# Rebuilding the projection stage and scoring four cosine heads at once in row tiles of 32 rows

## The reference

```python
xn = layernorm(x)
out = x + cosine_attention(xn) + block(xn)
# cosine_attention: 16 heads of 8; q and k scaled to unit length; scores = g_scale * q.k; softmax over all 1024 keys
# block: y = xn + causal_attention(rmsnorm(xn)*g1)   # 16 heads of 8, 4 key/value heads, rotary, softmax over keys <= query
#        y + moe(rmsnorm(y)*g2)                      # 4 experts of 384, the best 2 per token, silu(x w1)*(x w3) w2
```

## Time and profile before

| | us |
|---|---|
| median of 3 runs | 706.04 (703.66 to 708.68) |
| the profiled execution | 704.94 |
| its span, first to last instruction | 703.2 |

### The profile page before, as it was taken

How to read it: one execution, slowest core, us unless ns; L and a number is a source line. 1 busy time by engine, 2 the same in 40 slices (tenths; PEclk the granted TensorE clock), 3 DMA queues, 4 the chain that set the end, 5 groups by cost and what they waited for, 6 DMA issues and landing times.

```text
span 703.2 us, 11124 instructions
## 1 busy us (share of the span) xinstructions
PE 625.5 (89%) x4088; PEld 275.9 (39%) x4088; DVE 368.6 (52%) x1042; ACT 461.1 (66%) x520; POOL 106.1 (15%) x245
## 2 busy tenths in 40 slices
PE   0665887999999999999999999999998689999996
PEld 0433332333333333333333333333332445556654
DVE  6588385556556555555555654655521534344333
ACT  1444674888889888889888888988988332222221
POOL 8237000210210210130021021021002200000000
PEclk9979799999999999999999999999999889999999
DMA  3003411220311302124332030230000000000000
GB/s 84 4 1 61 70 20 17 47 45 4 61 19 28 58 6 47 30 34 92 100 52 38 10 62 12 35 48 16 1 3 1 1 0 1 15 1 16 0 16 15
DMA packets 19189, 20.61 MB, mean 29 GB/s; under 512 B 8128, under 2 KB 15552, under 8 KB 19136
## 3 DMA queue, kind: packets, MB, share of 16 engines
q1 hardware_dynamic: 16736, 19.62, 15.9%
q10 hardware_dynamic: 2400, 0.30, 0.3%
HBM read 3.84 MB, written 1.05 MB: 7 GB/s over the span
## 4 chain that ended last, share of the span: by engine, by line
PE 77%; DVE 12%; ACT 4%; issue 2%; SPq 2%; DMA 1%; POOL 0%; DVEq 0%; ACTq 0%
PE ps L1076 27%; PE ps L1057 19%; PE ps L1157 6%; PE ps L1008 6%; PE ps L1143 5%; PE ps L1144 5%; PE ps L1037 2%; DVE masked_scores L736 2%; DVE neg_piece L740 2%; PE ps L1031 2%; ACT probs L599 2%; DVE out_t L816 2%; SPq L361 2%; DVE probs L677 1%; DMA x_tok<-in_x 1%
## 5 line engine op out<-in xcount | busy, mean ns | idle before, releaser
L599 ACT ACTIVATE probs<-ps 128x1024 f32<-128x1024 f32 (+2 forms) x416 | 395.3, 991 | 80.1 <-PE ps L1057 75.8
L736 DVE CUSTOM_DVE_ANT_0 masked_scores<-ps,mask_q 128x384 bf16<-128x384 f32 (+3 forms) x256 | 111.6, 488 | 70.2 <-PE ps L1008 69.6
L1076 PE MATMUL ps<-probs,v_cos_pad 128*32 128x512 f32 x1024 | 138.1, 612 | 0.0
L1057 PE MATMUL ps<-q_cos_t,k_cos_t 64*128 64x512 f32 x512 | 122.9, 479 | 8.0 <-DMA q_cos_t<-parts_t_cos 6.2
L505 POOL TENSOR_SCALAR_AFFINE_SELECT probs<-probs 128x512 f32<-128x512 f32 x64 | 40.4, 637 | 412.9 <-ACT probs L599 412.9
L1057 PEld LDWEIGHTS ps<-q_cos_t,k_cos_t 64*128 64x128 f32 x512 | 48.2, 186 | 128.3 <-ACT probs L599 78.8
L740 DVE TENSOR_REDUCE neg_piece<-ps 128x1 f32<-128x512 f32 x128 | 82.1, 685 | 23.0 <-PE ps L1008 22.9
L637 ACT ACTIVATE probs<-ps 128x512 f32<-128x512 f32 x48 | 28.6, 597 | 96.3 <-PE ps L1144 84.9
L1076 PE MATMUL ps<-probs,v_causal_pad 128*32 128x512 f32 (+3 forms) x768 | 81.7, 498 | 0.3 <-POOL probs L505 0.3
L1057 PE MATMUL ps<-q_causal_t,k_causal_t 64*128 64x512 f32 (+3 forms) x384 | 73.5, 408 | 7.3 <-DMA q_causal_t<-neg_max_t 4.1
L1008 PE MATMUL ps<-k_causal_t,q_causal_t 33*128 33x512 f32 (+3 forms) x384 | 64.1, 371 | 17.3 <-DVE neg_piece L740 9.2
(11 more groups left out here) (131 smaller groups left out, 429.4 us busy)
## 6 DMA issues: line engine op xcount, KB each, us to landing
q_cos_t<-parts_t_cos SPq DMA_DIRECT2D x64, 64.0 KB
q_causal_t<-parts_t_rope SPq DMA_DIRECT2D x64, 64.0 KB
k_cos_t<-parts_t_cos SPq DMA_DIRECT2D x32, 64.0 KB
k_cos_t<-parts_t_cos SPq DMA_DIRECT2D x64, 32.0 KB
parts_cos<-in_w SPq DMA_DIRECT2D x2, 768.0 KB, 5.6
x_tok<-in_x SPq DMA_DIRECT2D x4, 256.0 KB, 4.4
k_causal_t<-parts_t_rope SPq DMA_DIRECT2D x16, 64.0 KB
k_causal_t<-parts_t_rope SPq DMA_DIRECT2D x32, 32.0 KB
```

Source lines behind the costliest of these rows:

```text
L599: act.activation(step_probs(n), step_scores(n), ACT.Exp).then_inc(probs_ready, 1)
L736: ins = dve.tensor_tensor_reduce(out=masked_scores[:, head % 2, at:at + keys], in0=scores, in1=mask_q[:, BANK - keys:BANK], scale=-1.0, sc ...
L1057: ins = pe.matmul(slot(n)[:, i, at:at + width], rounded(keys[:, j * P:(j + 1) * P]), rounded(queries[:, q0:q0 + width]), start=True, stop= ...
L1076: ins = pe.matmul(acc[32 * h:32 * h + 32, lo:], v, unit_probs(n)[:, h, lo:], start=j == 0, stop=True, skip_group_check=True)
```

## The change

**Projection.** `xn` is written at once (no staging, no copy on ACT). `xn_t`, `rope_in` and `rope_a` get two buffers. The second rope halves go from DVE to POOL. The clearing of the second pair of buffers on POOL moves behind the projection. 28 products of the identity come first on PE. The reciprocal of the norms is taken before their bound.

**First cosine rows.** Instead of the 20 DMAs, PE transposes the first parts into banks 6 and 7, ACT copies them, and products with matrices of zeros and ones (`choose_q`, `choose_k`, made on POOL) put the rows where they belong. ACT copies the first 512 tokens' rows, DVE the others. The loop starts when chunk 3's projections are read; ACT waits for the rest of chunk 3 at its steps 2, 4 and 6. The constant shift becomes the bias of the cosine exponentials. The rope jobs for iteration 1 go from steps 3 and 4 to 12 and 15 of iteration 0; its maxima start two steps earlier.

**Cosine steps from iteration 1 on** (`grouped`). A head takes 32 rows of the array instead of 64: pair (0,1) rows 0 and 64, pair (2,3) rows 32 and 96. There are three slots, banks 0 and 1, 2 and 3, 5 and 6, so step n waits for exponential n-3. All jobs in these steps use bank 7 alone. A value unit stands four steps behind its second score (three before). The 8 max jobs of two banks become 16 "one" jobs of one head and one bank, and some jobs stand behind the value unit of their step (place 1).

```diff
+def grouped(step):
+    return STEPS <= step < ITERS * STEPS and step % STEPS < COS_STEPS
...
+        last = it * STEPS + LAST_STEP[u]
+        step = last + (3 if on_diagonal(u) else 2)
+        if grouped(last) and grouped(last + 4):
+            step = last + 4
...
-EARLY_STEPS = (30, 32, 34, 35, 41, 42, 46, 48, 49, 51)
-MAX_STEPS = (8, 10, 12, 14, 16, 18, 19, 22)
+EARLY_STEPS = (32, 34, 35, 37, 41, 42, 46, 48, 49, 51)
+ONE_STEPS = ((1, 0), (3, 0), (5, 0), (7, 0), (7, 1), (9, 0), (11, 0), (11, 1), (13, 0), (15, 0), (15, 1), (17, 0), (19, 0),
+             (19, 1), (21, 0), (23, 0))
...
+        out += [(9, 1, ("out", it - 1, 3)), (23, 1, ("out", it, 0)), (25, 0, ("neg_max", it, 0))]
+        if more:
+            out += [(3, 1, ("rope", it + 1, 0)), (5, 1, ("rope", it + 1, 1))]
+            out += [(step, place, ("cos", it + 1, n)) for n, (step, place) in enumerate(((27, 1), (29, 1)))]
...
+SLOTS = ((0, 1), (2, 3), (5, 6))
+AUX_BANKS = (5, 6, 7)
...
+        elif grouped(step):
+            bank = AUX_BANKS[2]
+        else:
+            bank = AUX_BANKS[(AUX_BANKS.index(FILL_BANK[-1]) + 1) % 3]
...
+        SLOT.append(_step % 3 if grouped(_n) else _step % 2)
...
+                if kind == "one":
+                    pair, fill = MAX_JOBS[a // 2]
+                    i, at = a % 2, 0
+                    for t, key, keys, diagonal in MAX_FILLS[fill]:
+                        at += keys
+                        rows = slice(i * HEAD_ROWS, i * HEAD_ROWS + PRODUCT_ROWS)
+                        ins = pe.matmul(aux(m)[:, at - keys:at],
...
                     if kind == COS:
-                        keys, queries = k_cos_t[it % 2][rows, a, :], q_cos_t[it % 2][rows, a, :]
+                        first = cos_row(h) if grouped(n) else i * HEAD_ROWS
+                        rows = slice(first, first + (PRODUCT_ROWS if grouped(n) else HEAD_ROWS))
+                        keys, queries = k_cos_t[it % 2][rows, :], q_cos_t[it % 2][rows, a, :]
...
+            for half in range(2):
+                for i, choice in enumerate((choose_q[:, 0, :], choose_q[:, 1, :], choose_k[:, :])):
+                    if half:
+                        pe.wait_ge(first_rows_copied, i + 1)
+                    pe.matmul(ps[:, 5 + i, :], rounded(choice), rounded(parts_t["cos"][:, half * BANK:(half + 1) * BANK]),
+                              start=True, stop=True).then_inc(first_rows_in_psum, 1)
+            warm_up(WARM_UP, 4)
...
             for n in range(END + 1):
                 if n < ITERS * STEPS:
                     score_step(n)
-                for job in JOBS_AT.get(n, []):
+                for job in JOBS_AT.get((n, 0), []):
                     fill_banks(job)
                 if n in UNITS_AT:
                     value_unit(UNITS_AT[n])
+                for job in JOBS_AT.get((n, 1), []):
+                    fill_banks(job)
```

More of the change, by code:

```diff
@@ L128, in jobs_of @@
     if more:
[L129 to L134, removed]
+        out += [(step, 0, ("max", it + 1, n)) for n, step in enumerate(EARLY_STEPS)]
+    return sorted(out, key=lambda x: x[:2])
+JOBS = [(-1, 0, job) for job in FIRST_JOBS]
 for _it in range(ITERS):
-    JOBS += [(_it * STEPS + step, job) for step, job in jobs_of(_it)]
@@ L137 @@
-JOBS += [(END, ("out", ITERS - 1, 3))]
+    JOBS += [(_it * STEPS + step, place, job) for step, place, job in jobs_of(_it)]
+JOBS += [(END, 0, ("out", ITERS - 1, 3))]
 JOBS_AT = {}
[L139 to L147, removed]
-    FIRST_FILL.append(len(FILL_BANK))
[L149 to L153, removed]
+for _n, (_step, _place, _job) in enumerate(JOBS):
+    JOBS_AT.setdefault((_step, _place), []).append(_n)
@@ new lines, with _read, _add_job @@
+SLOTS = ((0, 1), (2, 3), (5, 6))
+AUX_BANKS = (5, 6, 7)
+SLOT, STEP_READ = [], []
+FIRST_FILL, FILL_BANK, FILL_READ = [], [], []
+_exps, _fills = {}, {}
+def _read(banks):
+    return max(_exps.get(bank, 0) for bank in banks), max(_fills.get(bank, 0) for bank in banks)
+def _add_job(n):
+    step, place, (kind, it, a) = JOBS[n]
+    FIRST_FILL.append(len(FILL_BANK))
+    for i in range(2 if kind == "max" else 1):
+        m = len(FILL_BANK)
+        if step < 0:
+            bank = 6 + m
+        elif grouped(step):
+            bank = AUX_BANKS[2]
+        else:
+            bank = AUX_BANKS[(AUX_BANKS.index(FILL_BANK[-1]) + 1) % 3]
+        FILL_READ.append(_read((bank,)))
+        FILL_BANK.append(bank)
+        _fills[bank] = m + 1
@@ L588, in _ @@
                 root_norms(c)
+            for half in range(2):
+                act.wait_ge(first_parts_in_psum, half + 1)
+                act.activation(rounded(parts_t["cos"][:, half * BANK:(half + 1) * BANK]), ps[:, 6 + half, :], ACT.Copy)\
+                   .then_inc(first_parts_copied, 1)
+            for i in range(3):
+                act.wait_ge(first_rows_in_psum, i + 1)
+                act.activation(first_rows(i, 0), ps[:, 5 + i, :], ACT.Copy).then_inc(first_rows_copied, 1)
             load_table(0, ACT.Exp)
@@ L787, in empty_banks @@
                         shift_of_maxima(m + 2, it)
+                elif kind == "one":
+                    pair, fill = MAX_JOBS[a // 2]
+                    empty_max(m, it, 2 * pair + a % 2, fill)
+                    if a == 2 * len(MAX_JOBS) - 1:
+                        shift_of_maxima(m + 1, it)
                 else:
```

369 lines of the change are left out of this document (224 added, 145 removed).

## The result

The changed kernel takes 752.33 us, median of four runs (737.19 to 761.8), the kernel before beside it 705.84: slower by a ratio of 1.050 (95% interval 1.038 to 1.063). I had forecast 708.6 and a range to 722. The ratio is taken over its two shorter runs alone, since the longer two lie further than usual above the shortest; here that spread is the kernel's own, as will be seen, so 1.050 is the low figure.

A forecast was written before the change was run, and what follows sets the result against it. PE's order of scores, fills and value units was taken to set the pace, with ACT's work as floor. From 704.94, minus 22 (projection and iteration 0) plus 25.7 (iterations 1 to 7) gave 708.6 us, range 690 to 722.

The forecast's parts named there:

- Projection and iteration 0: Front of the kernel: the causal start of iteration 0 and all behind it come 22 us earlier, bounds 15 and 27.
- the lower bound's cause: Projection: DVE's operations all take the longer of their times and POOL is late, so the gain is only 15 us.
- The rule that I had weighed and left out of the sum: Projection: two-SBUF-input DVE operations and SBUF-reading POOL operations exclude each other, making the gain 18 us instead of 22.
- Cosine and causal parts at the full clock: Iterations 1 to 7: cosine steps +2.7 and causal part +1.3 us an iteration, together +25.7 us for the loop.
- a round of bank 7: Cosine steps: fill, DVE read and hand-over take 1.41 or 1.48 us; 20 rounds make 29.0 us in steps 1 to 24.
- the forecast's own range: Whole kernel: 699 to 713 us, a change of under 1% as gain and loss nearly cancel; chance 0.42.
- The wait shows on PE in front of the first fill of the next unit: Cosine steps 1 to 24: waits on bank 7 hold up value unit and scores; 30.5 us instead of 26.0, +4.5.
- (a): Cosine steps: ACT, not bank 7, is the pace; rounds of 1.2 us give 673 us, 1.35 give 697; chance 0.25.
- (c): Cosine steps: the four heads do not run at once, 1.4 us more an iteration, 9 in seven: 718 us; chance 0.05.
- (b): Cosine steps: single-head fills cost more than half a pair, 0.06 to 0.1 us a round: 717 to 723 us; chance 0.28.
- The 0.90 us that I took for an exponential: Cosine steps 0 to 23 before the change: 26 exponentials in 23.35 us of ACT, 0.90 each, taken as the floor.

The follow-up runs named there:

- e3: Changed kernel with every cosine score product of iterations 1 to 7 issued twice: 734.18 us.
- e6: Changed kernel with its order, banks and waits, but cosine scores on 64 rows (two heads at once) and single fills on 33 rows: 725.95 us.
- e5: Changed kernel with two score slots instead of three and cosine-step fills on banks 5, 6 and 7 in turn, still 32-row tiles: 702.59 us.
- e9: e6 with two score slots as well and cosine-step fills on banks 5, 6 and 7 in turn: 708.35 us.
- e2: e1 with the score products of iterations 1 to 7 on 32 rows instead of 64: 723.58 us.
- e7: e2 with the paired fills of the cosine steps on 32 rows instead of 33: 698.24 us.
- e1: Changed kernel with the old order from iteration 1 (two slots, three banks, paired maxima jobs, 64-row scores), rebuilt projection and bias kept: 691.29 us, ratio 0.981 to before.
- e8: e1 without the bias on the cosine exponentials: 684.91 us, ratio 0.971 to the kernel before.

## Why the prediction was wrong

**Projection and iteration 0: right in kind, 22 against 19.4.** The first exponential came at 55.02 (54 forecast), iteration 0's causal start at 101.68 (98). At the causal start the gain is 120.13 - 101.68 = 18.4; the other 1.0 comes from iteration 0's causal part, which kept the full clock now and spent 3.0 us at 0.5 before, and that I had not forecast. DVE's first read of maxima was late, 61.10 instead of 58. The projection ran into the lower bound's cause, DVE and POOL together:

```profile
25.00 1.23 DVE L826 TENSOR_TENSOR probs<-probs 128x1024 f32<-128x1024 f32 x1
31.21 2.51 DVE L826 TENSOR_TENSOR probs<-probs 128x1024 f32<-128x1024 f32 x1
...
27.04 1.56 POOL L545 TENSOR_TENSOR probs<-probs,cos_t 128x640 f32<-128x640 f32 x1 [2.23 <-DVE probs L802]
...
31.10 1.53 POOL L552 TENSOR_TENSOR probs<-probs 128x640 f32<-128x640 f32 x1
32.59 2.54 POOL L558 TENSOR_TENSOR parts_rope<-probs,parts_rope 128x640 fp32r<-128x640 f32 x1
...
57.90 1.93 PE L1227 MATMUL ps<-probs,v_cos_pad 128*32 128x512 f32 x8
...
61.10 1.29 DVE L848 TENSOR_REDUCE neg_piece<-ps 128x1 f32<-128x512 f32 x2 [3.40 <-PE ps L1152]
```

The same DVE instruction takes 1.23 us while POOL is idle and 2.51, in all three later chunks, while POOL works. The 1.28 of difference, three times, is 3.8. POOL pays as well: L558 takes 2.54 here and 1.55 at 56.98, where DVE only copies out of PSUM. The rule that I had weighed and left out of the sum (the Trainium skill, SBUF — State Buffer, "SBUF: two separate sides") said 18 instead of 22; the measured 19.4, and still more the 18.4 at the causal start, lies nearer to it, and these rows agree with it. Only a part of the late first read is DVE's own: its row copies ended at 57.70, 1.3 us behind the 56.4 of the forecast. Then DVE waited 3.40 us for PE's first fill, where I had allowed 1.6: PE stood at granted clock 0.50 from 56.5 on, and the value unit ahead of that fill took 1.93 us.

**Cosine and causal parts at the full clock: right in kind, some 4 us short in all.** Iteration 6 has 39.0 and 23.1 us, I gave 38.5 and 22.9; its first 24 steps take 30.9 (30.5), the last eight 8.1 (8.0), a round of bank 7 1.40 (1.41). The waits stand where I put them, on DVE's reads: 0.67 to 1.12 on those of maxima, and three shorter ones of 0.24 to 0.41 on copies. The loop at the full clock loses 29.7, I said 25.7. With 737.19 - 24.9 = 712.3 such an execution would lie inside the forecast's own range of 699 to 713. That would be luck in part: the loop loses 4.0 more and the front gains 2.6 less than forecast, and without the 2.9 of the experts' part, which the sum did not have, it would be 715.2, above that range.

**The step that failed** is the sentence "The wait shows on PE in front of the first fill of the next unit, and since the value unit and the next scores stand behind it, ACT runs dry there": I priced the wait as time lost and nothing more, and carried every duration of the earlier trace rows, read at clock 1.00, over to a PE that now stops eight times in the twelve units of steps 0 to 23. The earlier trace rows show a granted clock of 1.00 in iteration 2, but 0.91 to 0.92 in the projection and iteration 0; I read past that column. The term that is missing, put at nothing without a reason, is the price of the low clock: 24.9 us in the profiled execution and, as an estimate, 40 in the median one (752.33 - 712.3). e3, which fills the waits, e6, which shortens them and doubles the rows, and e5, which takes them away, leave 13.7, 0 and 3.4 us at the low clock of the 71.7.

**The rivals.** (a), ACT as the pace, is out: ACT waits behind bank 7's rounds, 5.6 us in the first 24 steps of iteration 6. (c) is out: e5 and e9 differ by 1.4 an iteration in favour of four heads. (b) named a real price at another place. The single fills have the scores' shape, and pay nothing for it in the round of 1.40; where shapes alternate, in e2, a fill pays 0.28 for the change there and back (0.43 + 0.44 less 0.34 + 0.25), eight fills an iteration 2.2, and e2 less e7 is 60.1 - 58.0 = 2.1.

**The bias** is not in my sum. The 0.90 us that I took for an exponential was too low already: 23.35 us belong to the 24 exponentials of 24 steps, and two of the 26 that I counted only reach into the stretch. In steps 0 to 23 the rounds of bank 7 cover both. Exponentials in a row stand 1.01 us apart with it, in e1 (4.13 for four of 1.11 each, less 1.11, by 3), and 0.94 without, in e8 (3.84 for four of 1.02).

```profile
364.98 4.13 ACT L713 ACTIVATE probs<-ps,cos_shift 128x1024 f32<-128x1024 f32 x4 [0.37 <-PE ps L1211]
```

```profile
364.61 3.84 ACT L713 ACTIVATE probs<-ps 128x1024 f32<-128x1024 f32 x4 [0.47 <-PE ps L1211]
```

The Trainium skill (ScalarE: Activation LUTs, "What ACT_TABLE_LOAD costs") gives an operand of this kind 0.093 us; the trace shows 0.07 to 0.09 here, between 1.11 and 1.02 for one alone.

**What stays open.** Which iterations fall is not the same from one execution to the next, and why the clock stays low for 3.4 us in one and 30.7 in another was not settled; nor was why iterations with the same waits, as 5 and 6 of the profiled execution, differ. The times at the low clock come from one profiled execution of each kernel. e6 shortens the waits as well as doubling the rows, so the two shares in it are told apart only by e3 beside it and by the pair e7 and e1.

## What to carry to other kernels

A wait of TensorE can have two prices, its length and what it does to the granted clock of the products behind it; read PEclk beside PE's busy time for every stretch, and where a change puts waits into a stretch that ran at 1.00, give the low clock a price (here 0.35 to 0.37 us per microsecond at 0.5) and a chance. Buffers that one side of a pipeline gains, here a third slot of scores, come off another's, and a single bank that is filled and read in turn is a chain of its own, as long as fill, read and hand-over together. Products on fewer rows are no gain by themselves: here they gave 1.4 us an iteration in the new order (e5 against e9), nothing in the old one (58.0 in e7 and e1), and they cost 2.1 where the fills beside them had another tile shape (e2 against e7).

## What the runs showed of the hardware that I had not expected

- The same wait of 0.87 us was followed by value products of 1.07 us with 64-row tiles and of 1.94 with 32-row ones, while waits of 0.26 to 0.53 at that step of the iterations before left the clock alone with either.
- 448 products more made a kernel shorter (734.18 against 752.33 and 740.37 us), with 13.7 us at the low clock instead of 71.7 and 143.4.
- Going from a 32-row pair to a 33-row pair and back cost 0.28 us more than staying with one shape.
- Executions of one program spread from 727.62 to 763.52 us, in step with the granted clock of 0.953 to 0.894; kernels without waits on bank 7 or on 64 rows spread over 1 to 12 us.
